# Spiral scans and attention on one core: transfers at the edges reordered, the softmax shift brought to q by DMA

## What is computed

```python
def step(g, inp):                       # layers 0 and 3, once for each cell ci in spiral order
    ci, ni, nm, nc = inp
    local = g[:, ci, :]
    neigh = (g[:, ni, :] * nm[None, :, None]).sum(axis=1) / nc
    u = jnp.concatenate([local, neigh], axis=-1)
    y_sc = jnp.tanh(u @ w1 + b1) @ w2 + b2
    return g.at[:, ci, :].set(local + y_sc[:, None] * w_y[None, :]), None

q, k, v = x @ Wq + bq, x @ Wk + bk, x @ Wv + bv      # layers 1 and 2
attn = softmax(einsum('bnd,bmd->bnm', q, k))
out = gamma * einsum('bnm,bmc->bnc', attn, v) + x    # layer 2 has no gamma
```

## Time and profile before

| | |
|---|---|
| median of 3 runs | 4954.85 us (4953.62 to 4958.39) |
| profiled execution | 4950.95 us |
| its span, first to last instruction | 4948.9 us |
| TensorE busy | 4789.8 us, 97% |
| VectorE, ScalarE, GpSimd busy | 68%, 58%, 20% |
| first scan, attention, second scan | about 0 to 791, 814 to 4178, 4178 to 4927 us |

### The profile page before, as it was taken

One profiled execution on the slowest core, in us unless ns is written; L12 is line 12 of the kernel. 1 busy time (PEld: TensorE's weight loads), 2 busy tenths in 40 slices (PEclk: granted clock), 3 DMA queues, 4 the chain that ended last, 5 costly groups with the idle time before them and its releaser, 6 DMA issues.

```text
span 4948.9 us, 53360 instructions
## 1 busy us (share of the span) xinstructions
PE 4789.8 (97%) x16936; PEld 2292.7 (46%) x16936; DVE 3358.2 (68%) x5980; ACT 2886.9 (58%) x5225; POOL 985.5 (20%) x3206
## 2 busy tenths in 40 slices
PE   5999996999999999999999999999999998999997
PEld 2456653444444444444444444444444443445754
DVE  3888885666666666666666666666666663788876
ACT  1223222777777777777777777777777775223322
POOL 3454320110111111110111011101110112454431
PEclk9999997999999999999999999999999999999999
DMA  7569324111111111111111111111011413369625
GB/s 150 74 74 125 64 39 47 39 39 43 43 39 39 43 43 39 39 43 43 39 38 43 43 41 37 43 43 42 36 43 43 105 39 73 53 72 115 99 51 43
DMA packets 471686, 272.94 MB, mean 55 GB/s; under 512 B 437360, under 2 KB 438640, under 8 KB 471408
## 3 DMA queue, kind: packets, MB, share of 16 engines
q1 hardware_dynamic: 471408, 269.54, 27.2%
HBM read 135.29 MB, written 134.22 MB: 54 GB/s over the span
## 4 chain that ended last, share of the span: by engine, by line
PE 92%; DVE 4%; SPq 1%; DMA 1%; ACT 1%; issue 1%; POOL 0%; DVEq 0%; POOLq 0%; ACTq 0%
PE psum L912 37%; PE psum L885 9%; PE psum L856 9%; PE psum L837 8%; PE psum L847 8%; PE psum L947 6%; PE psum L934 6%; PE psum L898 5%; PE psum L962 3%; PE psum L923 3%; DVE shared L664 1%; DVE shared L639 1%; DVE shared L641 1%; SPq L397 1%; ACT shared L779 1%
## 5 line engine op out<-in xcount | busy, mean ns | idle before, releaser
L912 PE MATMUL psum<-shared 128*128 128x512 f32 x4096 | 1966.8, 603 | 1.3 <-DVE x L743 1.3
L701 DVE TENSOR_REDUCE top<-psum 128x1 f32<-128x1024 f32 x1024 | 1253.4, 1224 | 997.0 <-PE psum L898 997.0
L786 ACT ACTIVATE shared<-psum 128x512 f32<-128x512 f32 x2048 | 1110.9, 595 | 451.6 <-PE psum L885 447.9
L791 ACT ACTIVATE psum<-psum,top 128x1024 f32<-128x1024 f32 x1024 | 1115.1, 1089 | 362.0 <-DVE top L701 362.0
L912 PEld LDWEIGHTS psum<-shared 128*128 128x128 f32 x4096 | 718.2, 190 | 764.7 <-issue 509.1
L779 ACT ACTIVATE shared<-psum,b_col 128x320 f32<-128x320 f32 (+10 forms) x744 | 414.1, 568 | 1098.9 <-PE psum L847 1084.3
L520 POOL TENSOR_TENSOR shared<-arena 128x32 f32<-128x32 f32 (+6 forms) x1230 | 568.8, 492 | 894.3 <-PE psum L847 805.0
L534 POOL TENSOR_TENSOR ratio<-shrink,total 128x8 f32<-128x8 f32 x128 | 25.8, 201 | 2906.1 <-ACT shrink L802 2906.1
L837 PE MATMUL psum<-arena,w_own 128*128 128x320 f32 (+12 forms) x1672 | 541.5, 452 | 36.0 <-DMA arena<-x_cells 33.9
L847 PE MATMUL psum<-shared,w_sum 128*128 128x320 f32 (+10 forms) x1488 | 528.0, 477 | 49.5 <-POOL shared L520 32.7
L885 PEld LDWEIGHTS psum<-q,k 64*128 64x128 f32 x2048 | 190.7, 183 | 776.3 <-issue 677.4
(11 more groups left out here) (64 smaller groups left out, 3240.2 us busy)
## 6 DMA issues: line engine op xcount, KB each, us to landing
x<-layer_out SPq DMA_DIRECT2D x128, 512.0 KB, 3.2
layer_out<-x SPq DMA_DIRECT2D x128, 512.0 KB, 2.6
arena<-x_cells SPq DMA_DIRECT2D x8, 1520.0 KB, 12.9
layer_out<-arena SPq DMA_DIRECT2D x8, 1520.0 KB, 18.7
arena<-layer_out SPq DMA_DIRECT2D x8, 1520.0 KB, 14.0
y_cells<-arena SPq DMA_DIRECT2D x8, 1520.0 KB, 19.2
arena<-x_cells SPq DMA_DIRECT2D x4, 1504.0 KB, 17.9
layer_out<-arena SPq DMA_DIRECT2D x4, 1504.0 KB, 17.9
```

The lines of the kernel that those rows point to most:

```text
L701: nc.vector.reduce_max(top[i % 2][:, m:m + 1], rows_ps[m % 2][:], AX_X, negate=True).then_inc(row_max, 1)
L786: nc.scalar.activation(probs[u % PROBS], keys_ps[u % 2], ACT.Exp).then_inc(probs_ready, 1)
L791: nc.scalar.activation(rows_ps[m % 2][:], rows_ps[m % 2][:], ACT.Exp, bias=top[i % 2][:, m:m + 1], accum_out=total[i % 2][:, m:m + 1]).the ...
L912: nc.tensor.matmul(mix_ps, v[i % 2][:, tile(t)], probs[u % PROBS], start=(m == 0), stop=(m == MT - 1)).then_inc(mixed, 1)
```

## The change

It has four parts.

1. **Shift by DMA.** `spread_shift`, VectorE's `place_shift`, the strip and `ident_r` are gone. GpSimd writes `shift` as [128, high or low, 8] with two operations instead of four. SyncE issues `turn_shift` in slot 4, which writes it to DRAM as two rows of 1024 (2048 runs of 4 bytes), waits for it, and issues `place_shift` in slot 6, two transfers of two rows each from DRAM into rows 54 and 55 of each half of q. The first key energies of a job wait for both. To give time for this, row energies and their element work run three slots earlier (a job's last are in slot 1), the guess is in slot 2, keys of job j + 3 are made in slot 6, queries in slot 7 and in slot 1 (of job j + 2), values in slots 3 and 5. Slots 0, 2 and 4 have nothing extra. q and k have four buffers. The load of x moves from slot 4 to slot 3, its first use from slot 1 of the next job to slot 6 of the same job.
2. **Start.** Both scans' weights are issued by ScalarE. SyncE's first loads come in order of first use: chunks 0, 1, ENDING and 2 of A, then of B, then 3 to 6 of A, then of B. Chunk 1 is split in two of 64 and 31 cells. In the second scan B's first loads are split: 28 pictures at job 126, the last four when all is stored.
3. **Lead.** Stream A does levels 0 and 1 before B does level 0, and stays one level ahead; B does levels 62 and 63 one after the other. GpSimd's first sums of A in the second scan no longer wait for the last job.
4. **Tail.** The cells of levels 114 to 121 join the ENDING chunk (28 cells), the chunk before has 38 cells and ends at level 113. A's ENDING store is split: the first four pictures go first, and x of jobs 0 to 3 waits for these only.

```diff
+TAIL = 114
-    first = [0, 2]
-    for lv in range(2, LEVELS):
+    first = [0, 2, 6, 8]
+    for lv in range(8, TAIL):
...
+def turns():
+    lead = [(A, 0)]
+    for lv in range(JOIN):
+        lead += [(A, lv + 1)] * (lv + 1 < JOIN) + [(B, lv)]
+    return lead
...
+            if (g, k) == (A, ENDING):
+                sp.dma_start(scan_out[n][0:DEEP, :, chunk_cells(k)].rearrange("b c n -> c b n"),
+                             arena[:, 0:DEEP, chunk_places_of(k)]).then_inc(stored_first, 16)
+                b = slice(DEEP, IMAGES)
...
+        def turn_shift(i):
+            if is_job(i):
+                sp.wait_ge(shift_ready, i + 1)
+                positive(sp, shift_placed[i % 2], 32 * (i // 2))
+                sp.dma_start(shift_row[i % 2].rearrange("a (m p) -> p a m", p=P), shift[i % 2][:].bitcast(F32)
+                             ).then_inc(shift_turned[i % 2], 16)
+        def place_shift(i):
+            if is_job(i):
+                sp.wait_ge(shift_turned[i % 2], 16 * (i // 2 + 1))
+                for g in ROW_GROUPS:
+                    sp.dma_start(q[i % DEEP][g.start + TOP_ROW:g.start + TOP_ROW + 2, :].bitcast(F32), shift_row[i % 2]
+                                 ).then_inc(shift_placed[i % 2], 16)
...
-            load_scan_weights(0)
-            first_loads(0, A)
-            load_scan_weights(1)
-            first_loads(0, B)
+            for part in (FIRST_LOADS[:4], FIRST_LOADS[4:]):
+                for g in (A, B):
+                    for k in part:
+                        load(0, g, k)
             load_heads()
             follow(0)
-            for j in range(-3, JOBS + 1):
+            for j in range(-4, JOBS + 1):
                 for s in range(MT):
                     if s == 2:
                         store_image(j - 1)
+                    if s == 3:
+                        load_image(j + 3)
                     if s == 4:
-                        load_image(j + 3)
+                        turn_shift(j + 1)
+                    if s == 6:
+                        place_shift(j + 1)
                 if j == EARLY:
-                    first_loads(1, A)
-            for b in range(DEEP):
-                sp.wait_ge(out_stored[b], 16 * (JOBS // DEEP))
-            first_loads(1, B)
+                    out_stored_to(LAYERS * IMAGES - 1)
+                    for k in FIRST_LOADS:
+                        load(1, A, k)
+                if j == JOBS - 2:
+                    out_stored_to(JOBS - 1 - LATE_PICTURES)
+                    for k in FIRST_LOADS:
+                        load(1, B, k, slice(IMAGES, BATCH - LATE_PICTURES))
+            out_stored_to(JOBS - 1)
+            for k in FIRST_LOADS:
+                load(1, B, k, slice(BATCH - LATE_PICTURES, BATCH))
             follow(1)
...
         def attention(j, s):
             key_energies(j, 2 * s)
             key_energies(j, 2 * s + 1)
-            row_energies(j + 1 + (s + 3) // MT, (s + 3) % MT)
-            if s == 0:
-                spread_shift(j, 1)
+            row_energies(j + 1 + (s + 6) // MT, (s + 6) % MT)
+            if s == 6:
+                project_keys(j + 3)
+            if s == 7:
+                project_queries(j + 3, 0)
             if s == 1:
-                project_keys(j + 2)
-            if s in (2, 3):
-                project_queries(j + 2, s - 2)
-            if s in (5, 6):
-                project_values(j + 1, s - 5)
-            if s == 7:
-                spread_shift(j + 1, 0)
+                project_queries(j + 2, 1)
+            if s in (3, 5):
+                project_values(j + 1, s // 2 - 1)
```

More of the change, by code:

```diff
@@ L213 @@
 TOP_ROW = 54
-STRIP = P + MT
 EARLY = JOBS - 12
@@ L268, in cells, with loads_done @@
     return t[:, PICTURES[c], 0:level_size(lv)]
+FIRST_LOADS = sorted((k for k in range(ENDING + 1) if not earlier_tenants(k)),
+                     key=lambda k: (min(FIRST_READ[chunk_cells(k)]), -chunk_size(k) if k else -CELLS))
+LATE_PICTURES = 4
+def loads_done(n, g, k):
+    return 16 * (n + 1 + (n == 1 and g == B and k in FIRST_LOADS))
 def first_chunks(lv, first_use):
@@ L390, in wait_level, with load @@
             sp.wait_ge(updated[c], levels_done(n, c, lv))
-        def load(n, g, k):
+        def load(n, g, k, pictures=None):
             for e in earlier_tenants(k):
@@ L452, in store_image, with out_stored_to @@
                              ).then_inc(out_stored[i % DEEP], 16)
-        def first_loads(n, g):
-            for k in (0, ENDING, *range(1, ENDING)):
-                if not earlier_tenants(k):
-                    load(n, g, k)
+        def out_stored_to(i):
+            for b in range(DEEP):
+                sp.wait_ge(out_stored[b], 16 * ((i - b) // DEEP + 1))
         def follow(n):
@@ L528, in log_sums @@
             s, y, e = total[i % 2], guess[i % 2], shrink[i % 2]
-            first, second = (shift[i % 2][:, :, r + TOP_ROW:r + TOP_ROW + MT].rearrange("p h (m a) -> p h m a", a=2)
-                             for r in (0, ROW_GROUP))
-            value = ratio[:].rearrange("p (h m) -> p h m", h=2)
+            high, low = shift[i % 2][:, 0, :], shift[i % 2][:, 1, :]
             turn = LOG_TURNS * i
@@ L676, in scan @@
         def scan(n):
-            for c in (A, B):
-                sums(n, c, 1)
-            for lv in range(JOIN - 1):
-                for c in (A, B):
-                    add_steps(n, c, lv + 1)
-                    update(n, c, lv)
-                    if lv + 2 < JOIN:
-                        sums(n, c, lv + 2)
+            for c, lv in TURNS:
+                if lv > 0:
+                    add_steps(n, c, lv)
+                    update(n, c, lv - 1)
+                if lv + 1 < JOIN:
+                    sums(n, c, lv + 1)
             sums(n, BOTH, JOIN)
@@ L766, in _ @@
         prepare_scan(1)
-        for j in range(-2, JOBS + 1):
+        for j in range(-3, JOBS + 1):
             for s in range(MT):
@@ L823, in _ @@
         act.wait_ge(mixed, UNITS * JOBS)
-        for lv in range(LEVELS):
-            for c in streams_at(lv):
-                squash(1, c, lv)
+        scan(1)
     @block.tensor
@@ L949, in project_values @@
             mm.then_inc(v_raw, 1)
-        def spread_shift(i, h):
-            if not is_job(i):
-                return
-            if h == 0:
-                pe.wait_ge(shift_ready, i + 1)
-                pe.wait_ge(log_turn, LOG_TURNS * (i + 1))
-                pe.wait_ge(v_ready, 2 * i + 2)
-            else:
-                pe.wait_ge(shift_placed, 2 * i + 1)
-            for m in range(MT // 2):
-                mm = nc.tensor.matmul(misc_ps[:, tile(m)], shift[i % 2][:, h, 2 * m:2 * m + P], ident_r[:],
-                                      start=True, stop=True)
-            mm.then_inc(shift_rows, 1)
         def attention(j, s):
```

180 lines of the change are left out of this document (91 added, 89 removed).

## The result

The changed kernel takes **4928.72 us** (median of 5 runs, 4925.79 to 4936.38) against 4956.55 us before (5 runs): a ratio of 0.9948, 95% interval [0.9933, 0.9962]. It is faster by 0.5%, where 4820 us was forecast: the direction held, the size did not, and the range (4785 to 4880) missed it. The profiled execution took 4936.38 us, with a span of 4934.4 us; the one before had 4948.9. So of the 135 us forecast 14.5 came in the profiled execution, the slowest of the five, and 27.8 by the medians.

A forecast was written before the change was run, and what follows sets the result against it. It took attention as bound by TensorE's own work and the edges by transfers. -113 - 32 - 8 + 4 + 24 - 5 + 4 - 9 = -135 us gave 4816 on the profiled execution, 4820 on the median, range 4785 to 4880.

The forecast's parts named there:

- The 113 us: Attention: removing 1024 matmuls saves 0.88 us a job, 113 us over 128 jobs; a job becomes 25.14 us.
- the first rival: The 4-byte transfer is late, TensorE waits each job: 5061 us, chance 0.10; 4820 to 4955 us, chance 0.05.
- the way out: Writing the shift to DRAM in 2048 runs of 4 bytes: taken as 6 us, hidden up to 10.8, cost 0.
- the high end: Upper estimate for writing the shift to DRAM, from b_col's load at 5.4 ns a run: 12.7 us.
- the low end: Lower estimate for writing the shift to DRAM, from scan stores at 1.4 ns a run: 4.5 us.
- 8192 x 1.4 + 1.6 = 13: End of the span: two transfers of 4096 runs instead of four, 22.6 us after the last update become 13: -9 us.
- Half of 16384 runs is 11.5 us less at 1.4 ns: End of the first scan: the tail is 8192 runs, with x queued behind them: -8 us (-3 to -11).
- Filling: +4: Filling the attention pipeline: the first L885 comes later by the new path, partly covered by other TensorE work: +4 us (0 to +7).
- The block at job 116: Eight loads of A in SyncE's queue delay x; TensorE stands 22 us, plus 2 for the restart: +24 us (0 to +30).
- a forecast of 32: Start: near B issued at 38 us, 26 us earlier, and 6 us of A's work already done: -32 us (-20 to -36).
- the +4 for the join: Join of the streams: B does its last two levels alone, 2 us a scan: +4 us (+1 to +6).
- -5 for the edge: Edge to the second scan: near B no earlier, as stores queue behind loads, but A's 6 us of work done: -5 us.

The follow-up runs named there:

- the other session: The changed kernel again with nothing edited, timed in another session: 4883.23 us (4 runs), ratio 0.9859 to the kernel before.

## Why the prediction was wrong, and where it was right

**The matmuls removed: right, but not cashed.** A plain slot takes 2.57 us and a job that doesn't wait 25.15 us. The 113 us are there in the run with the turned shift. That the key energies would then wait for the shift was the first rival (0.10 for a large excess, 0.05 for a small one), and it came in its milder form. That the direction held is in part luck: by the prediction's own sum the sign turns at 11.9 us, and the way out took 11.8.

**The way out: the step that failed.** It was "I take 6, nearer to the row of the same direction and a large count". Measured were 11.8 us; the high end, 12.7 from b_col's median, was near, and the low end, 4.5, is what 2048 such runs take when no two share a line. The scan stores that gave the low end write runs of 200 and 64 bytes, so that hardly any line is written twice; the shift writes each line 16 times. I had read the count and the direction off the rows and not where the writes fall. With the limit at 11.4 (the way back was 0.6 us shorter than taken) the excess was small: the job is 0.41 us longer than 25.14, 60 us saved in 128 jobs of the profiled execution instead of 113, and 106 in the other session. Over the whole attention TensorE waited 61.9 us for it. The table's -18 is made so: 127 jobs of 25.14 us are 3192.8; 24.8 for x, and 61.9 - 5.6 = 56.3 for the shift (the 5.6 stand before job 0) give 3273.9; 11.7 us up to 3285.6 I can't put on a row (7 of them in the middle stretch, where 76.4 jobs are 31 us longer and the waits are 24.4).

The Trainium skill, "DMA: Bandwidth & Descriptors", section Specifications, says that below 512 bytes a transfer is done as a read-modify-write. The trace agrees in so far as the step was dearer than I took it; that a read is the reason no run here shows. The profile's count of bytes read from HBM grew by 2.10 MB, 137.39 against 135.29, and the way back alone reads that much (256 transfers of 8 KB). The rule also makes no difference between 4.5 and 11.3 us, which were measured on runs of one size. It was a reason for more than 0.15 on the late transfer.

**Tail and end: failed too.** The step was "8192 x 1.4 + 1.6 = 13", and its sibling "Half of 16384 runs is 11.5 us less at 1.4 ns". It priced runs by their count. Chunk and tail meet at cell 996 now, 16 bytes into a line, where before they met at 1008, at byte 4032 = 63 x 64. So -9 became +10.3 and -8 became +13.4. With the meeting point at 992 they are 8.4 us in place of the forecast 13, and 11.6 in place of 15 (23.0 - 8). So the price by run lacked a condition. No row that I had put beside the prediction shows it, for no boundary at the old tail broke it, but the trace of before does. Its stores of cells 672 to 768 (both ends on a line) and of 127 to 217 (both inside one), each with 4096 runs, land so:

```profile
layer_out<-arena SPq DMA_DIRECT2D x2, 1536.0 KB, 10.4
layer_out<-arena SPq DMA_DIRECT2D x2, 1440.0 KB, 23.5
```

The larger one is the quicker. Three of A's stores in the first scan, beside which only B's store of the same cells is in the queue, say it more cleanly: 7.6 us with both ends on a line (cells 672 to 768), 12.6 with one end inside (768 to 863), 15.1 with both inside (863 to 958). It could have been read before the change was made.

**Filling: +4 was +10.7.** I let all but the path be covered by TensorE's other work. The run with the turned shift leaves 6 us of it where the path is short, so I put that part to the new order, which has the row energies three slots earlier and more of them ahead of job 0; no run shows that by itself.

**The block at job 116: right.** "TensorE stands for 22 us", and 2 for the restart; it was 24.8. The queue held 31.61 us for eight loads (34 forecast) and 5.63 for the store, as the earlier trace rows had it:

```profile
3841.50 31.61 SPq L422 DMA_DIRECT2D arena<-layer_out  x8
3873.16 5.63 SPq L490 DMA_DIRECT2D layer_out<-x  x1
3882.94 0.34 SPq L469 DMA_DIRECT2D x<-layer_out  x1
```

**Start, join and edge: right in size.** Near B stands at 42.3 us where 38 was forecast, and the first scan became 26.3 us shorter for a forecast of 32, less half of the +4 for the join: 30. From the last job's key energies to the last update it is 2.0 - 6.5 = -4.5 us, where -5 for the edge and half of +4 for the join were forecast. The stores did queue behind B's loads, as the second set of rows of the edge shows.

In sum: of the 120 us missing, 53 are the way out's in the jobs, 21 the end of the first scan, 19 the end of the span, 7 the filling, 4 the start with the join; the other 16 lie in the attention before and after the middle stretch. The waits for the shift there are 31.9 us (21.2 up to 1667, less the 5.6 ahead of job 0, and 16.3 from 3619), 11 more than 0.41 us in each of these 51 jobs; the other 5 are of the 11.7 us without a row. The two large ones, the way out and the tail, are each taken back by an experiment.

## What to carry to other kernels

Before merging or moving a store of short runs, work out whether its boundaries fall on multiples of 64 bytes, and how many runs write to the same 64 bytes; here four cells of shift in a boundary were worth 51 us, and one matmul that turned 2048 runs of 4 bytes into 16 of 512 took the way out from 11.3 to 1.3 us. When a change puts a new path beside the bound, compare its length with the limit in tenths: at 0.1 us of slack, another session moves the kernel by 1%. And a load that may go early is best issued one to a stage and not eight in a row, since the queue behind it stands still.

## What the runs showed of the hardware

- **Stores and lines.** In the run with the tail at cell 992, A's and B's tail stores are 8192 runs of 128 bytes, which start and end on lines; they need at most 8.4 us with their landing. With 1.6 us taken off for a small transfer's landing, that is (8.4 - 1.6) / 8192 = 0.8 ns a run, an estimate. The changed kernel's 8192 runs of 112 bytes, which start inside a line, end 32.9 us after the last update; a part of this is the store before them, which ends inside the same lines and was still landing when they were issued (issued from 744.98 us on in the first scan, landed after 18.5 and 34.0 us, the tail issued at 764.71). Loads of the same chunks, whose runs lie across lines as well, land much sooner: 15.1 us against 26.6 for the stores, by the changed kernel's DMA issues (count, KB each, median us to landing).

```profile
arena<-x_cells SPq DMA_DIRECT2D x6, 1520.0 KB, 15.1
layer_out<-arena SPq DMA_DIRECT2D x6, 1520.0 KB, 26.6
```

- **Writes of 4 bytes.** 2048 of them land after 4.5, 5.4 or 11.3 us, by 1, 4 or 16 to a line.
- **Strided 4-byte reads into one row**: with each value on a line of its own, the four transfers of 1024 runs on the way back, issued one after the other, landed after 17.4 us (median) where the 2048 runs of the way out took 4.5. How much of that is the reading, and how much the writing into one row of q, no run tells. By that kernel's DMA issues:

```profile
q<-shift_row SPq DMA_DIRECT2D x512, 4.0 KB, 17.4
shift_row<-shift SPq DMA_DIRECT2D x128, 8.0 KB, 4.5
```

- **A small transfer to DRAM** of 16 runs of 512 bytes lands 1.3 us after its start. That is 10 us under the way out that it replaced.
- **Landing differs between sessions** by 0.5 us (11.8 against 11.3, the latter on two chips), while every other stage is the same within about 2 us.
